# A gated attention-and-feed-forward layer on one core: another order of loads and instructions, a mask table, idle transposes, and the last batch's feed-forward by halves

## The chip, the cores and the metric

The kernel runs on one core of a Trainium2 chip, written directly for the engines: TensorE (PE) multiplies and transposes, VectorE (DVE), ScalarE (ACT) and GpSimd (POOL) do elementwise work, SyncE (SP) issues most DMAs. The metric is the time of one execution on the device in microseconds; lower is better. A time given for a kernel is the median of its runs.

## What is computed

x and ctx are 8 batches of 512 tokens by 256 features. The weights are wq, wk, wv, wo (256x256), pos_bias (512x512), w1 (256x1024), w2 (1024x256), w_gate, w_up (1024x256) and w_down (256x1024), with their bias rows. All is float32.

```
def aft_local(emb, ...):                 # T = 512 tokens, window S = 64
    q, k, v = emb @ wq + bq, emb @ wk + bk, emb @ wv + bv
    mask = abs(i - j) < 64
    w = pos_bias * mask                  # zero outside the band, still summed
    ek, ew = exp(k - max_over_tokens(k)), exp(w - max_over_j(w))
    num, den = ew @ (ek * v), ew @ ek    # ew is 512x512
    return (sigmoid(q) * num / den) @ wo + bo

def block1(x, ctx):
    emb = layer_norm(x) + ctx
    a   = layer_norm(aft_local(emb) + emb) * gamma + beta
    ff  = relu(a @ w1 + b1) @ w2 + b2
    return layer_norm(ff + a) * gamma + beta

def block2(x):                           # int8-like activations, ternary weights
    bit(x, w) = quantised(x) @ quantised(w).T
    # weight scale: mean(|w|), then round and clip to -1, 0, 1
    return bit(silu(bit(x, w_gate)) * bit(x, w_up), w_down)

x = x + tanh(g_xattn) * block1(layernorm(x), ctx)
x = x + tanh(g_ffn)   * block2(layernorm(x))
```

## The kernel before

**Tiling.** A batch is four tiles of 128 tokens. Work goes batch by batch in a software pipeline: while TensorE does the feed-forward products of batch b, the other engines prepare the attention of batch b+1 and the second block of batch b-1 or b-2. Every fp32 product is split: each operand has an upper part (`_hi`, written by ScalarE) and a lower part (`_lo`, the rest, written by VectorE), and three products hi·hi, lo·hi and hi·lo are added (helper `product`, L2444). So each operand passes PSUM, ScalarE, VectorE, and back to TensorE.

**Order.** There is no scheduler: for each engine a list of calls is written out by hand, such as `hidden(0, 3)`, and semaphore counts tie the lists together. An engine runs its list strictly in order, so a call that waits holds everything behind it. PSUM has eight banks; the table `BANK` says which bank each step of each batch uses, and `bank_wait` makes TensorE wait until the bank's last reader is through.

**Steps of the first block,** in their order per batch, with the line that the profile shows. Layer norm: `tile_stats` (DVE L1550), `mean_variance` (L1558), `rsqrt` on GpSimd (L530 to L535), `normalise` (ACT L847). `embed` adds ctx (POOL L540). `emb_rows` transposes it (PE L2452), `emb_upper` and `emb_lower` split it (ACT L861, DVE L1563). `keys_T` and `max_row` (L2461, L2478) give the largest key per feature, used by `bias` (DVE L1584). `queries` and `keys_values` are products (L2444) with wq and with wk, wv; `half_sigmoid` (ACT L868), `add_bias` (DVE L1591), `exp_keys` (ACT L874), `weighted` (DVE L1597) and `e_upper`, `e_lower` (ACT L881, DVE L1602) follow. `attend` multiplies the banded part of ew with ek and ek*v, 256 columns at a time; outside the band ew is constant per row, so `key_sums` (L2510), `sum_upper` and `sum_lower` (ACT L888, DVE L1607) and `attend_far` (L2518) add the rest. `gated`, `inverse` (DVE L1611), `divided` and `y_upper`, `y_lower` (ACT L894, DVE L1628) finish, `project` multiplies with wo. After the next layer norm, `n1_rows` transposes (L2535), `n1_upper` and `n1_lower` split (ACT L900, DVE L1640), and `hidden(b, m)`, m from 0 to 7, makes 128 of the 1024 hidden features for all 512 tokens; `hidden_upper`, `hidden_whole` (ACT L907, L912) and `hidden_lower` (DVE L1646) feed `feed_forward(b, m)`. h_hi and h_lo are rings of four.

**Tables made once, early.** `positions_T` transposes exp(w - max) (PE L2411), after the band's zeros are set (`masks`, POOL L504, L507), the row maximum is taken (`position_max`, DVE L1496) and the exponential (`exp_positions`, ACT L810); `ewT_upper`, `ewT_lower` split it (ACT L815, DVE L1504), `far_row` and `far_weights` make the constant part. `beta_w1` (PE L2428) and `b1_whole` give beta @ w1 + b1. The weights are split by `wkv_upper` (ACT L777), `wkv_lower` (DVE L1476), `w1_upper`, `w1_lower` (ACT L798, DVE L1490) and so on. Each of w_gate, w_up, w_down (n = 0, 1, 2) is quantised by `sum_of_magnitudes` (ACT L822), `bit_scale` (DVE), `bit_round` (ACT L829), `bit_clip` (DVE L1539), `bit_whole` (ACT L837) and a DMA transpose `bit_rows`.

**Second block.** `second_residual`, layer norm, `n2_gamma` (POOL L572), `first_sum` (POOL L579, which writes the tile `x1`, one buffer for all batches), layer norm, `token_quantise` (ACT L919), the transposed activations (by DMA, and on TensorE for batch 7), `gate` and `up` (PE L2592), `silu`, `product` and `product_scale` (DVE L1683 to L1701), the quantised product, `down` (PE L2614) and `output(b, t)` (DVE L1707), which reads x1 and writes the result.

## Time and profile before

| what | value |
|---|---|
| median of 3 runs | 529.32 us |
| lowest and highest | 527.03 and 531.65 us |
| the profiled execution | 531.71 us |
| its span | 530.0 us |
| busy, share of the span: PE, DVE, ACT, POOL | 90%, 82%, 70%, 46% |
| the chain that ended last, by engine | PE 17%, ACT 4%, DMA 4%, issue 3%, POOL 2%, DVE 2% |

The profile is of one execution. Its span runs from the first to the last recorded instruction; the execution's own time is 1.7 us longer. Busy shares are averages over stages that differ, so the rows below are read by stretch and not by share. In a timeline row, the numbers are the start and the length in us, then the engine, the line of the kernel, the operation, what it writes and reads, and in square brackets how long the engine had been idle and who released it. A row of busy time per stretch has start and end, the length, the busy time and (x) the instructions of PE, PEld (weight loads), DVE, ACT and POOL, then the granted TensorE clock, the busy share of the DMA engines and GB/s; where it was asked for TensorE alone, only that engine stands in it.

### The profile page before, as it was taken

What the parts mean: (1) busy time and instruction counts of PE and PEld (TensorE: products, weight loads), DVE (VectorE), ACT (ScalarE), POOL (GpSimd) and SP (SyncE); (2) the same over time, 40 slices, a digit from 0 to 9 for tenths busy, and PEclk for the clock granted to TensorE, in tenths of its full rate; (3) what the DMA queues carried; (4) which work ended last, traced back from release to release, by engine and by line L of the source; (5) the groups of instructions that cost most, each with busy time, mean ns of one, the idle gap of its engine ahead of it and who ended that gap; (6) DMA issues with size and microseconds to landing.
All of it is one profiled execution on the core that took longest, in us unless ns stands there. A gap on an engine that the chain in (4) does not pass through costs nothing. (4 is left out here: it accounts for less than half of the span.)

```text
span 530.0 us, 9499 instructions
## 1 busy us (share of the span) xinstructions
PE 478.4 (90%) x2912; PEld 390.5 (74%) x2912; DVE 432.7 (82%) x992; ACT 372.8 (70%) x594; POOL 245.8 (46%) x386
## 2 busy tenths in 40 slices
PE   0499579999999999999999999999999999897394
PEld 0389468998887888779877888788778987775132
DVE  3676985958798989898989898998899789768474
ACT  2467874556868957886788769787768776886563
POOL 2863016318712575354743484348415903574410
PEclk9997998999999999999999999999999999999577
DMA  5965142101301233023302331222123202232301
GB/s 175 276 205 179 28 69 64 41 0 41 80 22 21 61 90 91 16 54 91 90 12 40 80 92 51 40 62 76 44 41 81 61 0 39 61 71 52 79 0 41
DMA packets 69328, 36.01 MB, mean 68 GB/s; under 512 B 47008, under 2 KB 68768, under 8 KB 69280
## 3 DMA queue, kind: packets, MB, share of 16 engines
q1 hardware_dynamic: 68160, 35.14, 26.1%
q8 instruction: 25, 0.41, 0.3%
q10 hardware_dynamic: 1120, 0.27, 0.2%
q14 instruction: 23, 0.19, 0.1%
HBM read 20.46 MB, written 4.19 MB: 47 GB/s over the span
## 5 line engine op out<-in xcount | busy, mean ns | idle before, releaser
L530 POOL TENSOR_TENSOR mv<-mv,cols 128x2 f32<-128x2 f32 x64 | 12.5, 195 | 176.6 <-DVE mv L1558 176.6
L2444 PE MATMUL ps<-w_hi,h_hi 128*128 128x256 f32 x256 | 75.8, 296 | 0.0
L2444 PE MATMUL ps<-w_lo,h_hi 128*128 128x256 f32 x256 | 71.6, 280 | 0.0
L2444 PE MATMUL ps<-w_hi,h_lo 128*128 128x256 f32 x256 | 71.5, 279 | 0.0
L907 ACT ACTIVATE h_hi<-ps,cols 128x512 fp32r<-128x512 f32 x64 | 43.8, 685 | 19.8 <-PE ps L2444 15.5
L1611 DVE RECIPROCAL ps<-ps 128x512 f32<-128x512 f32 x16 | 53.6, 3355 | 0.6 <-PE ps L2518 0.6
L2444 PE MATMUL ps<-n1T_hi,w_hi 128*128 128x512 f32 x128 | 51.3, 401 | 0.8 <-DVE n1T_lo L1640 0.8
L2444 PE MATMUL ps<-n1T_lo,w_hi 128*128 128x512 f32 x128 | 50.6, 396 | 0.0
L2444 PE MATMUL ps<-n1T_hi,w_lo 128*128 128x512 f32 x128 | 50.6, 395 | 0.0
L2444 PEld LDWEIGHTS ps<-w_hi,h_hi 128*128 128x128 f32 x256 | 48.3, 189 | 2.8 <-DVE h_lo L1646 0.2
L2444 PEld LDWEIGHTS ps<-w_lo,h_hi 128*128 128x128 f32 x256 | 48.3, 188 | 1.1
L1646 DVE TENSOR_TENSOR h_lo<-ps,h_hi 128x512 fp32r<-128x512 f32 x64 | 42.6, 682 | 7.5 <-ACT ps L912 7.1
L2444 PEld LDWEIGHTS ps<-w_hi,h_lo 128*128 128x128 f32 x256 | 48.2, 188 | 0.0
L1683 DVE TENSOR_TENSOR work<-work,ps 128x1024 f32<-128x1024 f32 x32 | 38.9, 1215 | 11.1 <-issue 8.1
L2614 PE MATMUL ps<-wdT,w_bit 128*128 128x256 bf16 x256 | 36.7, 291 | 12.1 <-DMA w_bit<-place_c 8.2
L847 ACT ACTIVATE work<-work,nmr,rstd 128x256 f32<-128x256 f32 x64 | 34.9, 595 | 14.3 <-POOL nmr L535 14.2
L953 ACT ACTIVATE work<-ps,cols 128x1024 f32<-128x1024 f32 x32 | 35.6, 1112 | 13.2 <-DVE work L1683 7.7
L533 POOL TENSOR_TENSOR rstd<-mv,cols 128x2 f32<-128x2 f32 x64 | 44.5, 695 | 0.0
L1550 DVE BATCH_NORM_STATS2 st<-work 128x6 f32<-128x256 f32 x96 | 36.5, 414 | 9.6 <-POOL work L579 9.2
L2444 PE MATMUL ps<-ew_hi,e_hi 128*128 128x256 f32 x128 | 38.6, 302 | 3.6 <-DVE e_lo L1602 3.2
L912 ACT ACTIVATE ps<-ps,cols 128x512 f32<-128x512 f32 x64 | 41.9, 657 | 0.0
L2614 PEld LDWEIGHTS ps<-wdT,w_bit 128*128 128x128 bf16 x256 | 24.3, 103 | 23.0 <-DMA w_bit<-place_c 11.2
(175 smaller groups left out, 1460.9 us busy)
## 6 DMA issues: line engine op xcount, KB each, us to landing
emb<-in_ctx_dram SPq DMA_DIRECT2D x16, 256.0 KB, 3.1
x_in<-in_x_dram SPq DMA_DIRECT2D x16, 256.0 KB, 2.9
work<-in_x_dram SPq DMA_DIRECT2D x8, 512.0 KB, 3.9
out_dram<-work SPq DMA_DIRECT2D x16, 256.0 KB, 2.1
work<-in_L_xattn_w_dram SPq DMA_DIRECT2D x2, 1024.0 KB, 8.4
work<-in_L_ffn_w_gate_dram SPq DMA_DIRECT2D x1, 1024.0 KB, 5.6
work<-in_L_ffn_w_up_dram SPq DMA_DIRECT2D x1, 1024.0 KB, 5.6
place_c<-in_L_ffn_w_down_dram SPq DMA_DIRECT2D x1, 1024.0 KB, 4.9
```

What stands on the lines that cost most here:

```text
L530: pool.tensor_tensor(mv[:, n, c, 1], mv[:, n, c, 1], eps_col[:, c], ALU.add).then_inc(power_step[n].sem, 1)
L533: pool.tensor_tensor(rstd[:, n, c], mv[:, n, c, 1], minus_half[:, c], ALU.pow).then_inc(power_step[n].sem, 1)
L847: last = nc.scalar.activation(dst[:, t, :], src[:, t, :], ACT.Identity, bias=nmr[:, n, t:t + 1], scale=rstd[:, n, t:t + 1])
L907: nc.scalar.activation(h_hi[:, m % RING, :], bank(b, "h", m), ACT.Relu, bias=b1_col[:, m:m + 1]).then_inc(h_hi_ok.sem, 1)
L912: nc.scalar.activation(bank(b, "h", m), bank(b, "h", m), ACT.Relu, bias=b1_col[:, m:m + 1]).then_inc(h_relu_ok.sem, 1)
L953: nc.scalar.activation(sg, bank_pair(b, "gate", t), ACT.Silu, scale=sgate[:, t:t + 1]).then_inc(sg_ok.sem, 1)
L1550: nc.vector.bn_stats(st6[:, n, t, :], src[:, t, :]).then_inc(stats[n].sem, 1)
L1611: nc.vector.reciprocal(bank(b, "den", h), bank(b, "den", h)).then_inc(rden_ok.sem, 1)
L1646: nc.vector.tensor_tensor(h_lo[:, m % RING, :], bank(b, "h", m), h_hi[:, m % RING, :], ALU.subtract).then_inc(h_lo_ok.sem, 1)
L1683: nc.vector.tensor_tensor(prod[t % 2].rearrange("p (a n) -> p a n", a=2), sg.rearrange("p (a n) -> p a n", a=2), bank_pair(b, "up", t), AL ...
L2444: last = nc.tensor.matmul(dst, lhsT, rhs, start=(i == 0 and not begun), stop=(i == n - 1 and ends))
L2614: last = nc.tensor.matmul(bank(b, "down", t)[:, 0:D].rearrange("p (k n) -> p k n", n=P), hqT[t % 2][:, k, :], wdT[:].rearrange("p (k j) n ...
```

## The change

**Loads.** x and ctx of batch 0 are fetched first, then the weights wq, wo, wk, wv, then the two bias rows bk and bv (`fetch_bias`, moved from ScalarE's queue to SyncE's), and the positions only after those. w1 is fetched after w2 and, by a new semaphore `masked`, not before both halves of the mask are applied. w_up and w_down are fetched after `bit_rows(0)`.

Here is how SyncE's list begins before; `place_c` holds the positions, `work` takes the weights.

```order
L338 DMA place_c<-in_L_xattn_pos_bias_dram 128x2x384
L305 DMA emb<-in_ctx_dram 128x2x256
L299 DMA x_in<-in_x_dram 128x2x256
L305 DMA emb<-in_ctx_dram 128x2x256
L299 DMA x_in<-in_x_dram 128x2x256
L338 DMA work<-in_L_xattn_wk_dram 128x2x256
L338 DMA work<-in_L_xattn_wv_dram 128x2x256
L338 DMA bo_all<-in_L_xattn_bo_dram 128x256
```

And after:

```order
L316 DMA x_in<-in_x_dram 128x2x256
L322 DMA emb<-in_ctx_dram 128x2x256
L316 DMA x_in<-in_x_dram 128x2x256
L322 DMA emb<-in_ctx_dram 128x2x256
L355 DMA work<-in_L_xattn_wq_dram 128x2x256
L355 DMA work<-in_L_xattn_wo_dram 128x2x256
L355 DMA work<-in_L_xattn_wk_dram 128x2x256
L355 DMA work<-in_L_xattn_wv_dram 128x2x256
L355 DMA bk_all<-in_L_xattn_bk_dram 128x256
L355 DMA bias_all<-in_L_xattn_bv_dram 128x256
L316 DMA x_in<-in_x_dram 128x2x256
L355 DMA place_c<-in_L_xattn_pos_bias_dram 128x2x384 x2
```

The positions went from the first place to the twelfth row, and both halves of x stand ahead of every weight.

**The mask.** GpSimd no longer writes zeros into the loaded positions. `band(h)` fills a table `in_band` with ones and sets zeros in it by two selects, which needs no load; `position_max` on VectorE multiplies the positions by it and then takes the maximum.

**Idle transposes.** TensorE runs 50 transposes of the identity into bank 7 before its first useful one. Their result is never read. The `queries` of batch 0 now stand ahead of all `keys_values`, and `positions_T` and `beta_w1` later.

TensorE's list begins so before; `ident` is the identity, `embT` the transposed emb.

```order
L2411 MATMUL ps<-ident,place_c 128x128 x2
L2452 MATMUL ps<-ident,emb 128x128 x8
L2461 MATMUL ps<-embT_hi,wkv_hi 128x512 x4
L2444 MATMUL ps<-wkv_hi,embT_hi 128x512
L2444 MATMUL ps<-wkv_lo,embT_hi 128x512
L2444 MATMUL ps<-wkv_hi,embT_lo 128x512
```

And after:

```order
L2686 MATMUL ps<-ident 128x128 x50
L2509 MATMUL ps<-ident,emb 128x128 x8
L2518 MATMUL ps<-embT_hi,wkv_hi 128x512 x4
L2501 MATMUL ps<-embT_hi,wq_hi 128x512
L2501 MATMUL ps<-embT_lo,wq_hi 128x512
L2501 MATMUL ps<-embT_hi,wq_lo 128x512
```

In front of emb's eight transposes the two of the positions are gone and the 50 idle ones stand; behind `keys_T` come products with wq and no longer with wk and wv.

**Quantised weights.** Only w_gate is quantised before batch 1's attention. The steps for w_up and w_down now stand between the hidden products of batch 0, on ScalarE, VectorE and TensorE (`total`). w1 and w2 are split in two calls each, later.

ScalarE's list after batch 0's keys, before. L822 is `sum_of_magnitudes`, L829 `bit_round`, L888 `sum_upper(0)`, L861 `emb_upper(1, h)`.

```order
L822 ACTIVATE wdT,cols<-work 128x2048
L888 ACTIVATE esum<-ps 128x512
L822 ACTIVATE wdT,cols<-work 128x2048
L861 ACTIVATE embT_hi<-ps 128x512
L829 ACTIVATE work<-work,cols 128x2048
L822 ACTIVATE wdT,cols<-place_c 128x2048
L861 ACTIVATE embT_hi<-ps 128x512
L829 ACTIVATE work<-work,cols 128x2048
```

After, in batch 0's hidden stage. L845 is `sum_of_magnitudes`, L931 and L936 are `hidden_upper` and `hidden_whole`, L917 `y_upper(1, 0)`.

```order
L936 ACTIVATE ps<-ps,cols 128x512
L845 ACTIVATE wdT,cols<-work 128x2048
L931 ACTIVATE h_hi<-ps,cols 128x512
L917 ACTIVATE y_hi<-ps 128x512
L936 ACTIVATE ps<-ps,cols 128x512
L845 ACTIVATE wdT,cols<-place_c 128x2048
L931 ACTIVATE h_hi<-ps,cols 128x512
```

The second and third sums stood around batch 1's first `emb_upper`; now they stand between batch 0's `hidden_upper` calls.

**n1 by token halves.** `n1_rows`, `n1_upper`, `n1_lower` take a pair of token tiles and both feature halves, in all batches, where before they took a feature half and all tokens.

**The last batch by halves.** For batch 7 (`HALVED`) `hidden` runs for tokens 0 to 255 with m from 0 to 7 and then for tokens 256 to 511, and `feed_pair` after it; each half starts as soon as its own n1 is there, and `second_residual` waits for its own half.

**The tail.** GpSimd runs `first_sum(7, 0)` straight behind `n2_gamma(7, 0)`; `gate(7, 2)` stands before `up(7, 2)`; on VectorE `output(7, 1)` stands before `product_scale(7, 3)`.

GpSimd's list near its end, before. L572 is `n2_gamma` (the first for batch 7, tiles 0 and 1), L579 `first_sum(7, 0)`, L584 and L585 `quantise`, L530 to L535 `rsqrt`.

```order
L572 TENSOR_TENSOR work<-work,g_all 128x512
L584 TENSOR_TENSOR cols<-cols 1x1
L585 TENSOR_SCALAR work<-work,cols 128x1024
L530 TENSOR_TENSOR mv<-mv,cols 128x2
L531 TENSOR_TENSOR mv<-mv,cols 128x2
L533 TENSOR_TENSOR rstd<-mv,cols 128x2
L535 TENSOR_TENSOR nmr<-mv,rstd 128x2
L572 TENSOR_TENSOR work<-work,g_all 128x512
L579 TENSOR_TENSOR work<-work 128x512
```

After (L596 `n2_gamma`, L603 `first_sum`):

```order
L608 TENSOR_TENSOR cols<-cols 1x1
L609 TENSOR_SCALAR work<-work,cols 128x1024
L596 TENSOR_TENSOR work<-work,g_all 128x512
L603 TENSOR_TENSOR work<-work 128x512
L554 TENSOR_TENSOR mv<-mv,cols 128x2
L555 TENSOR_TENSOR mv<-mv,cols 128x2
L557 TENSOR_TENSOR rstd<-mv,cols 128x2
L559 TENSOR_TENSOR nmr<-mv,rstd 128x2
```

`first_sum(7, 0)` no longer stands behind a `rsqrt` and the second `n2_gamma`.

Between the ends, in batches 1 to 6, neighbouring calls change places, of which the one used below is on VectorE: `y_lower(b, 1)` stands behind `hidden_lower(b-1, 5)` and `hidden_lower(b-1, 6)` and not ahead of them. The `BANK` table is new throughout. The core of the diff:

```diff
-VECTORS1, VECTORS2 = 6, 7
+VECTORS1, VECTORS2 = 4, 7
+WARM_UP = 50
+HALVED = (7,)
+HALF = (slice(0, 2 * P), slice(2 * P, T))
...
-    ("embT", 0): (0, 4, 4, 1, 0, 2, 4, 0), ("embT", 1): (1, 5, 2, 1, 7, 7, 7, 7), ("kT", 0): (0, 1, 2, 7, 7, 7, 7, 4),
+    ("embT", 0): (0, 7, 6, 5, 0, 4, 0, 4), ("embT", 1): (1, 3, 7, 0, 7, 6, 7, 6), ("kT", 0): (2, 1, 1, 5, 3, 3, 3, 0),
...
+            def fetch_bias():
+                fetch("bias", bk_all[:], bk[None, :].to_broadcast([P, D]))
+                fetch("bias", bias_all[:, D:2 * D], bv[None, :].to_broadcast([P, D]))
+
             def fetch_w1():
+                sp.wait_ge(masked, 2)
                 fetch("w1", raw_w1, w1.rearrange("(k p) n -> p k n", p=P))
...
-            def masks(h):
-                w = half(raw_pos, h)[:, :, KEYS[h][0]:KEYS[h][1]]
-                pool.wait_ge(load[f"pos{h}"], 16)
+            def band(h):
+                c, n, w = KEYS[h][0], KEYS[h][1] - KEYS[h][0], in_band[:, 2 * h:2 * h + 2, :]
+                pool.memset(w, 1.0).then_inc(mask_ok, 1)
+                pool.wait_ge(mask_ok, 3 * h + 1)
                 pool.affine_select(out=w, in_=w, compare_op=ALU.is_ge, fill=0.0, ...
...
             def position_max(h):
-                dve.wait_ge(mask_ok, 2 * h + 2)
+                w = half(raw_pos, h)[:, :, KEYS[h][0]:KEYS[h][1]]
+                dve.wait_ge(load[f"pos{h}"], 16)
+                dve.wait_ge(mask_ok, 3 * h + 3)
+                nc.vector.tensor_tensor(w, w, in_band[:, 2 * h:2 * h + 2, :], ALU.mult).then_inc(masked, 1)
+                dve.wait_ge(masked, h + 1)
+                nc.vector.tensor_reduce(wmax[:, 2 * h:2 * h + 2], w,
                                         AX.X, ALU.max).then_inc(wmax_ok, 1)
...
-            def hidden(b, m):
-                wait(pe, n1T_lo_ok, b, 2)
+            def hidden(b, m, p=0, c=slice(0, T)):
+                wait(pe, n1T_lo_ok, b, p + 1 if b in HALVED else 2)
                 pe.wait_ge(lo_ok["w1"], ND)
-                bank_wait(b, "h", m)
-                product(bank(b, "h", m), [(w1_hi[:, k, c], w1_lo[:, k, c], n1T_hi[:, k, :], n1T_lo[:, k, :])
+                bank_wait(b, "g" if p else "h", m)
+                product(h_bank(b, m, p)[:, c], [(w1_hi[:, k, r], w1_lo[:, k, r], n1T_hi[:, k, c], n1T_lo[:, k, c])
...
+            def feed_pair(b, m, p):
+                wait(pe, h_lo_ok, b, NH * p + m + 1)
+                if m == 0:
+                    bank_wait(b, "f", p)
+                feed_tiles(b, m, (2 * p, 2 * p + 1)).then_inc(f_ps.sem, 1)
...
             pe.wait_ge(const_ok, 5)
+            for _ in range(WARM_UP):
+                nc.tensor.transpose(ps[:, 7, 0:P], ident[:], ident[:])
             pe.wait_ge(dve_const_ok, 5)
-            positions_T(0)
             emb_rows(0, 0)
             emb_rows(0, 1)
             keys_T(0, 0)
             keys_T(0, 1)
+            queries(0, 0)
+            queries(0, 1)
+            max_row(0)
             keys_values(0, 0)
...
             y_lower(4, 0)
-            token_max(2, 1)
-            y_lower(4, 1)
...
             hidden_lower(3, 5)
             hidden_lower(3, 6)
+            y_lower(4, 1)
...
             n2_gamma(7, 0)
-            quantise(6, 2)
+            first_sum(7, 0)
             rsqrt(7, 2, 1)
+            rsqrt(7, 3, 0)
             n2_gamma(7, 1)
-            first_sum(7, 0)
```

## Rows read from the trace of the kernel before

**Rows 1.** Busy time per stretch: all engines
```profile
0.00:90.00 90.00, 61.51 (x323) 51.74 (x324) 61.84 (x143) 52.56 (x79) 39.54 (x59) 0.94 0.51 141
90.00:480.00 390.00, 387.08 (x2430) 323.05 (x2429) 340.90 (x772) 293.11 (x481) 192.64 (x301) 1.00 0.22 54
480.00:530.00 50.00, 29.80 (x163) 15.68 (x162) 29.98 (x79) 27.09 (x35) 13.61 (x26) 0.73 0.18 43
90.00:130.00 40.00, 39.99 (x255) 35.54 (x254) 32.14 (x75) 24.68 (x45) 16.28 (x31) 1.00 0.10 29
```

**Rows 2.** Timeline of TensorE at the start
```profile
11.78 0.66 PE L2411 MATMUL ps<-ident,place_c 128*128 128x128 f32 x2 [11.78 <-ACT place_c L810]
19.42 1.97 PE L2452 MATMUL ps<-ident,emb 128*128 128x128 f32 x8 [6.98 <-POOL emb L540]
```

**Rows 3.** TensorE's busy time per stretch, two stretches of 128x512 products
```profile
24.17:28.28 4.11, 4.11 (x9) 1.00 1.09 374
28.28:30.39 2.11, 2.11 (x11) 1.00 0.80 315
```

**Rows 4.** Timeline of VectorE at the start
```profile
8.36 0.75 DVE L1550 BATCH_NORM_STATS2 st<-x_in 128x6 f32<-128x256 f32 x2 [4.31 <-DMA x_in<-in_x_dram]
13.56 0.75 DVE L1550 BATCH_NORM_STATS2 st<-x_in 128x6 f32<-128x256 f32 x2 [3.08 <-DMA x_in<-in_x_dram]
16.00 2.25 DVE L1476 TENSOR_TENSOR wkv_lo<-work,wkv_hi 128x1024 fp32r<-128x1024 f32 x1 [1.40 <-ACT wkv_hi L777]
```

**Rows 5.** Timeline from 31 to 50 us
```profile
31.56 1.29 DVE L1591 TENSOR_TENSOR kv_f<-ps,bias_all 128x512 f32<-128x512 f32 x2
...
35.50 4.17 PE L2428 MATMUL ps<-cols,work 128*128 128x1 f32 x32
...
36.09 2.46 DVE L1490 SCALAR_TENSOR_TENSOR w_lo<-work,cols,w_hi 128x1024 fp32r<-128x1024 f32 x2
...
42.26 0.38 ACT L815 ACTIVATE ew_hi<-ps 128x256 fp32r<-128x256 f32 x1 [4.68 <-PE ps L2411]
...
49.57 0.69 DVE L1607 TENSOR_TENSOR esum<-ps,esum 32x512 fp32r<-32x512 f32 x1 [0.25 <-ACT esum L888]
```

**Rows 6.** Lines by form: ns min/median/max, first to last start, form and count
```profile
L1539 DVE TENSOR_SCALAR work<-work x2: 1215/1216/1216, 59.1 to 65.3; 128x2048 f32<-128x2048 f32 x2
...
L822 ACT ACTIVATE wdT<-work x2: 1898/1900/1903, 46.2 to 49.4; 128x2048 bf16<-128x2048 f32 x2
```

**Rows 7.** Loads: KB each and median us from issue to landing
```profile
work<-in_L_ffn_w_up_dram SPq DMA_DIRECT2D x1, 1024.0 KB, 5.6
```

**Rows 8.** Timeline from 63 to 88 us
```profile
63.90 0.47 PE L2444 MATMUL ps<-wkv_hi,embT_hi 128*128 128x512 f32 x1 [3.15 <-ACT work L868]
...
79.26 0.51 PE L2444 MATMUL ps<-ew_hi,e_hi 128*128 128x256 f32 x1 [2.36 <-DVE e_lo L1602]
79.28 0.66 DVE L1602 TENSOR_TENSOR e_lo<-ps,e_hi 128x512 fp32r<-128x512 f32 x1
...
87.58 0.47 PE L2444 MATMUL ps<-n1T_hi,w_hi 128*128 128x512 f32 x1
```

**Rows 9.** TensorE's busy time per stretch, around batch 1's key sums
```profile
79.26:83.82 4.56, 4.56 (x18) 0.63 0.41 78
83.82:84.88 1.06, 1.06 (x10) 1.00 0.00 0
```

**Rows 10.** Timeline around the projection of batch 4
```profile
262.18 0.68 DVE L1628 TENSOR_TENSOR y_lo<-ps,y_hi 128x512 fp32r<-128x512 f32 x1
...
263.04 0.36 PE L2444 MATMUL ps<-wo_hi,y_hi 128*128 128x256 f32 x1
```

**Rows 11.** Timeline of the tail
```profile
491.61 0.86 DVE L1707 SCALAR_TENSOR_TENSOR work<-ps,cols,work 128x256 f32<-128x256 f32 x2
...
493.53 1.27 POOL L579 TENSOR_TENSOR work<-work 128x512 f32<-128x512 f32 x1
...
499.91 0.47 DVE L1707 SCALAR_TENSOR_TENSOR work<-ps,cols,work 128x256 f32<-128x256 f32 x1
```

More of the change, by code:

```diff
@@ L1582, in bias @@
                 wait(dve, mrow_ps, b, 1)
+                dve.wait_ge(load["bias"], 32)
                 wait(dve, kvb_ok, b, 0)
@@ L2780, in _ @@
             max_row(3)
-            queries(3, 1)
+            feed_forward(1, 5)
             gate(0, 2)
@@ L3085, in _ @@
             attend_far(7, "num", 0)
-            attend_far(7, "den", 0)
-            feed_forward(6, 2)
+            hidden(6, 2)
             attend(7, "den", 1, 2)
+            attend(7, "den", 1, 3)
+            attend_far(7, "den", 1)
             attend(7, "num", 1, 1)
```

1146 lines of the change are left out of this document (598 added, 548 removed), and 19 rows, old and new, of the table BANK.

## The prediction

> **What bounds the kernel now.** I read the busy time by stretch first [rows 1]. From 90 to 480 us TensorE is busy for 387.08 of 390 us at the full clock, so nothing that only re-orders work there can win more than 3 us. The two ends are different: in the first 90 us TensorE is idle for 28.5 us, in the last 50 for 20.2 us, and the granted clock there means 0.94 and 0.73. The timeline then says what is late at the ends.
>
> At the start the matmuls wait 6.98 us for `emb` [rows 2]. Ahead of it stand the second half of x (VectorE waits 3.08 us for it until 13.56) and additions on GpSimd [rows 4]. Then nine 128x512 products start in 4.11 us, 0.46 us each, and from 28.28 nine more in 2.11 us, 0.23 each (the count of 11 holds two that reach over the edges) [rows 3]. That is 1.2 and then 2.4 GHz, though the clock column reads 1.00 in both: this early I read the clock from spacing. From 31.56, where batch 0's first `add_bias` runs on VectorE [rows 5], the chain is mostly VectorE's: e_lo, the position tables, the key sums (ended at 50.26, 49.57 + 0.69), the division, then the same for batch 1, ending with the last e_lo(1,3) at 79.94 (79.28 + 0.66) [rows 5, 8]. The weight-quantisation steps (sum of magnitudes, round, clip, whole) are packed in between [rows 6]. At 87.58 the first hidden product of batch 0 starts [rows 8], and TensorE is full from there.
>
> **Part 1, loads, mask and ScalarE's order up to `add_bias(0,0)` (31.56).** x and ctx of batch 0 now go first, without the 384 KB of positions and without the two bias rows on ScalarE's queue. Before, the load issued third (x's first half) was there at 8.36 and the fifth (its second half) at 13.56 [rows 4]. Now the second half of x is third: there at about 8.5. From its landing to the transposes of emb it took 19.42 - 13.56 = 5.9 us [rows 2, 4]; `normalise(0,0,1)` now also stands behind `wq_upper`, which waits for the fifth load. With 0.2 for that, the transposes of emb run at 14.6: 4.8 us earlier. The mask costs GpSimd two fills and four selects before x is there: nothing. It costs VectorE two products of 768 elements. A 1024-element product takes 2.46 / 2 = 1.23 us [rows 5], so about 0.9 us each. `keys_T`, both `queries` and `max_row` now run before any `keys_values`: 4 + 12 products, of which I take ten at 0.45 and six at 0.23, so 17.0 + 5.9 + 0.6 = 23.5, and `bias(0)` at 24. Behind it stand `mean_variance` (0.3) and `position_max(1)` (0.9 + 0.9 + 0.3): `add_bias(0,0)` at 26.7. Term: **-4.9 us**, from -7 to 0 (weights as late as before, wkv_lo at 16.00 [rows 4]).
>
> The 50 idle transposes start at about 1.6. A transpose of this shape takes about 0.25 us at the low level (8 in 1.97 [rows 2]), so they end between 7 and 14, before the 14.6. They take nothing. Do they give the full clock? After two transposes at 11.78 and 6.98 us idle the next products ran at 1.2 GHz [rows 2, 3]; after 2.36 us idle at 79.26 they did too, with a granted clock of 0.63 [rows 8, 9]. With 1 to 7 us of idle time behind the last idle transpose I expect the low level again, so zero. By a warm start instead, 8 x 0.1 + 10 x 0.22 = 3.0 us would be saved; that is a rival. The Trainium skill (TensorE: Matmul & The Clock Gate, "HAM oscillation") says that an idle gap throttles the clock again, which speaks against this edit; the 6.98 us of this trace agree, and the sum is the same without the page.
>
> **Part 2, from `add_bias(0,0)` to batch 0's key sums (31.56 to 50.26).** Before, this took 18.7 us. VectorE's own work in it, without w1's lower half (2.46 us [rows 5]), is four `add_bias` of 0.6 (1.29 for two [rows 5]), four e_lo of 0.6, four products of 0.33, four lower tables of 0.36, statistics (0.9) and 2.1 for the far weights: 10.6 us. The rest was TensorE's and ScalarE's doing: `beta_w1` held TensorE for 4.17 us ahead of the products, and ScalarE waited 4.68 us for the position tables [rows 5]. Now w1 and `beta_w1` come later and all tables are transposed before the first `attend`. I keep 2.4 us of waits between the engines: 13.0 us, **-5.7 us** (-7 to -3).
>
> **Part 3, from there to e_lo(1,3) (50.26 to 79.94).** Two clips of 1.22 us [rows 6] leave VectorE, as do two short scales (0.7) and 1.9 us of idle time; half of w1 (1.2), b1, statistics (1.0) and a wait for the first numerator (1.1) come in: -1.5. TensorE now has gaps of some 2 us here and will run `queries(1)` and `keys_values(1)` in part at 1.2 GHz. The row for that is the stretch from 79.26: nine products of 256 columns and eight of 512 took 4.56 us [rows 9]; at 0.12 (nine in 1.06 [rows 9]) and 0.23 they take 2.9, so 1.7 us are lost. I charge 1.5. Term: **0 us** (-3 to +3).
>
> **Part 4, to the feed-forward of batch 0.** ScalarE gets what left part 3: two sums of magnitudes (1.90 each [rows 6]), and two rounds and two wholes of the same 2048 elements, together 12 us, among the hidden products. From 90 to 130 us ScalarE is busy for 24.68 of 40 us and VectorE for 32.14 [rows 1]; with 12 and 2.5 more, 37 and 35 of 40 fit. The loads of w_up and w_down now wait for w1's lower half, about 70, and need 5.6 us [rows 7]: there before `sum_of_magnitudes(1)` at 77. I find no product that waits for these steps by more than 0.3 us. The 1.7 us of low clock in front of the key sums disappear and the last heads' products (0.8) come behind the first hidden ones, which moves work, not time. Term: **-1.5 us** (-2 to +4).
>
> **Part 5, the middle.** The batch order is changed in small ways. The place with the least room: `y_lower(b,1)` of batch 4 ended at 262.86 (262.18 + 0.68) and `project` started at 263.04 [rows 10]. It now stands behind two more h_lo (0.6 each) and a later reciprocal; I get 264.8. TensorE reaches `project` after one more group of transposes and one more `feed_forward` (0.4 + 1.4): 264.85. It just fits. Term **+0.5** (-1 to +6).
>
> **Part 6, the tail.** A half of tokens costs TensorE nothing: 256 columns follow each other at 0.12 us and 512 at 0.23 [rows 3, 9]. ScalarE pays 16 x 0.12, VectorE 16 x 0.06 us, beside TensorE's work. Batch 7's first half now finishes early, but x1 has one buffer: `first_sum(7,0)` needs `output(6,1)` (491.61 + 0.86 = 492.47) and ran at 493.53 behind an `n2_gamma` [rows 11]. It goes ahead of it now: -1.0. The second half needs `output(6,3)`, which ended at 500.38 (499.91 + 0.47 [rows 11]), and from there SiLU, product, maximum and scale per tile are a chain of VectorE and ScalarE to the end. gate before up gives up to 0.9, the earlier start 1, and `product_scale(7,3)` behind `output(7,1)` takes 0.5 back. Term **-1.5 us** (-3 to +1).
>
> **Sum.** -4.9 - 5.7 + 0 - 1.5 + 0.5 - 1.5 = -13.1 us. The profiled execution took 531.71 (span 530.0), so 518.6. It lay 2.4 us above the median 529.32 of the three runs (527.03 to 531.65); against the median: 516.2, rounded to **516.5**.
>
> **The rivals.**
> (a) The start comes earlier but is handed back: the quantisation steps meet batch 0's hidden stage. h_hi and h_lo pass through one in-order queue each, and a 2 us step ahead of them costs as much. With three of the six steps uncovered, +6, the time is 522.5. Against it: 15 us of room on ScalarE [rows 1].
> (b) The loads gain nothing, because many transfers share the queues: part 1 is 0, the time is 521.4.
> (c) The idle transposes hold the clock: 3.0 us more, 513.5. For it: a gap of 3.15 us at 63.90 was followed by a 128x512 product of 0.47 us, the full level [rows 8].
> (d) Slower: `project` waits for y_lo in each of the five middle batches. It decides from a wait of 2.6 us per batch, where 5 x 2.6 = 13 us eats the gain. Such a wait dropped the clock at 79.26 and cost 1.7 more [rows 8, 9]; 5 x (2.4 + 1.7) = 20.5 gives 537. For it: the room is 0.1 us by my reckoning. Against it: VectorE would have to be 2.4 us later than its rows.
> wkv_lo, 1024 elements with both inputs in SBUF, took 2.25 us beside `embed` [rows 4], against 1.23 alone. If both mask products met GpSimd's work they would cost 1.5 us more, inside part 1's bounds; in my order GpSimd waits then. The Trainium skill (SBUF — State Buffer, "Who interferes with whom") says the same of a VectorE instruction with two SBUF inputs and a GpSimd one that reads; the row agrees.
>
> **How the numbers follow.** Forecast 0.62, (c) 0.10, (a) 0.12, (b) 0.10, (d) 0.06. The bounds of the parts together, less than their plain sum since they are independent, give 516.5 + 7 and - 5.5; this takes in (a), (b) and (c), so the range is 511 to 523.5. Three runs tell a change from none at about 1%, 5.3 us: below 524.0 is faster. That is the forecast, (a), (b) and (c) but for their outer parts, 0.86; (d) half decided leaves 0.09 within 1%, 0.05 slower.
>
> **What would show it.** In the profile after: emb's transposes at 14 to 16 us, the first products behind them at 0.43 to 0.46 spacing (0.23 means rival c); `add_bias(0,0)` at 25 to 28; e_lo(1,3) near 68; the first hidden product near 73; TensorE over 0.98 busy from 75 to 465. Then ScalarE's steps of 2 us lie between hidden ones with no wait of TensorE behind them, and the wait of `project` for y_lo is under 0.3 us. The last product_scale to the end is as long as before. The prediction is wrong if VectorE's stretch between the key sums of batches 0 and 1 is longer than its rows (waits for TensorE at the low clock), or if the middle has gaps.

## The result, and the profile after

The changed kernel took 511.43 us (median of 4 runs, 510.02 to 513.87), the kernel before 530.32 us in the runs beside it (527.03 to 531.65). The ratio is 0.9652, 95% interval 0.962 to 0.9684: 3.5% faster, where 2.4% was forecast. On two other chips, later, it took 512.99 against 528.82 us (0.9693, 0.9659 to 0.9727) and 511.27 against 529.27 us (0.9673, 0.9643 to 0.9703).

The two profiled executions differ by more than the medians do: 531.71 and 510.02 us, spans 530.0 and 508.3. The first lay above its median and the second below. So the trace has 21.7 us to explain where the medians have 18.9. I laid the same marks in both traces, starts of an instruction unless "end" is said:

| mark | before | after | difference | of the stretch |
|---|---|---|---|---|
| transposes of emb, batch 0 | 19.42 | 14.32 | -5.1 | |
| `add_bias(0,0)` | 31.56 | 25.33 | -6.2 | -6.2 |
| `sum_lower(0)`, end | 50.26 | 37.84 | -12.4 | -6.2 |
| last e_lo of batch 1, end | 79.94 | 65.66 | -14.3 | -1.9 |
| first hidden product of batch 0 | 87.58 | 70.91 | -16.7 | |
| first hidden product of batch 1 | 123.02 | 108.11 | -14.9 | -0.6 |
| first hidden product of batch 5 | 346.77 | 331.62 | -15.2 | -0.2 |
| first hidden product of batch 7 | 453.06 | 436.68 | -16.4 | -1.2 |
| end of the span | 530.0 | 508.3 | -21.7 | -5.3 |

The mark at batch 0's hidden product alone would mislead: it came 16.7 us earlier, but part of batch 1's attention now stands behind it, and one mark later 14.9 are left.

First the busy time per stretch, which answers to [rows 1].

```profile
0.00:75.00 75.00, 65.66 (x372) 57.17 (x373) 64.47 (x138) 42.36 (x74) 41.30 (x62) 0.91 0.54 155
75.00:465.00 390.00, 388.77 (x2480) 324.88 (x2480) 345.31 (x792) 306.82 (x504) 193.87 (x302) 1.00 0.24 57
465.00:509.00 44.00, 26.11 (x161) 15.12 (x159) 28.21 (x74) 26.33 (x35) 13.59 (x26) 0.79 0.22 49
```

The middle is as full as it was, 388.77 of 390 us, and it begins 15 us earlier. VectorE is busy for 64.47 of the first 75 us (86%), where it was for 61.84 of 90: most of what the start gained is idle time that VectorE no longer has.

The timeline of TensorE at the start answers to [rows 2, 3].

```profile
1.62 7.90 PE L2686 MATMUL ps<-ident 128*128 128x128 f32 x50 [1.62 <-POOL ident L617]
14.32 1.94 PE L2509 MATMUL ps<-ident,emb 128*128 128x128 f32 x8 [4.80 <-POOL emb L564]
...
19.24 0.63 PE L2501 MATMUL ps<-embT_lo,wq_hi 128*128 128x512 f32 x1
19.67 0.49 PE L2501 MATMUL ps<-embT_hi,wq_lo 128*128 128x512 f32 x1
20.00 0.40 PE L2501 MATMUL ps<-embT_hi,wq_hi 128*128 128x512 f32 x1
```

The 50 idle transposes end at 9.52, TensorE is idle for 4.80 us, and emb's eight transposes take 1.94 us, as long as before (1.97). The products start 0.43 us apart (19.24, 19.67) and 0.23 apart from 20.00. TensorE had been at the full level in between: of the idle transposes, 16 start in the 3.4 us up to 5.00 and 24 in the 3 us after that.

VectorE's timeline answers to [rows 4, 5, 8].

```profile
8.83 0.75 DVE L1595 BATCH_NORM_STATS2 st<-x_in 128x6 f32<-128x256 f32 x2 [1.07 <-DMA x_in<-in_x_dram]
...
23.25 0.93 DVE L1539 TENSOR_TENSOR place_c<-place_c,work 128x768 f32<-128x768 f32 x1
24.21 0.95 DVE L1541 TENSOR_REDUCE cols<-place_c 128x2 f32<-128x768 f32 x1
...
25.33 1.28 DVE L1637 TENSOR_TENSOR kv_f<-ps,bias_all 128x512 f32<-128x512 f32 x2
...
37.15 0.69 DVE L1653 TENSOR_TENSOR esum<-ps,esum 32x512 fp32r<-32x512 f32 x1 [0.63 <-ACT esum L911]
...
44.07 3.36 DVE L1657 RECIPROCAL ps<-ps 128x512 f32<-128x512 f32 x1
47.34 1.27 DVE L1608 TENSOR_TENSOR embT_lo<-ps,embT_hi 128x512 fp32r<-128x512 f32 x2
```

x's second half is there at 8.83, `add_bias` follows `position_max(1)` without a gap, and the lower part of emb for batch 1 follows the second reciprocal without one.

ScalarE's list in batch 0's hidden stage, with two of the moved steps (L845 `sum_of_magnitudes`):

```profile
75.14 1.91 ACT L845 ACTIVATE wdT<-work 128x2048 bf16<-128x2048 f32 x1
76.94 0.20 ACT L845 ACTIVATION_READ_ACCUMULATOR wdT<-work 128x1 f32 x1
77.03 0.69 ACT L931 ACTIVATE h_hi<-ps,cols 128x512 fp32r<-128x512 f32 x1
...
78.08 0.68 ACT L936 ACTIVATE ps<-ps,cols 128x512 f32<-128x512 f32 x1
78.65 1.93 ACT L845 ACTIVATE wdT<-place_c 128x2048 bf16<-128x2048 f32 x1
```

And the waits of TensorE in the changed kernel, us in total, times, longest:

```profile
PE ps L2680 <- DMA w_bit<-place_c: 6.5, 4, 2.1
PE ps L2509 <- POOL emb L564: 4.8, 1, 4.8
PE ps L2680 <- ACT w_bit L990: 4.0, 3, 1.4
PE ps L2658 <- ACT xqT L969: 2.5, 2, 1.5
PE ps L2686 <- POOL ident L617: 1.6, 1, 1.6
PE ps L2518 <- ACT embT_hi L884: 1.4, 2, 0.7
PE ps L2509 <- DVE cols L1566: 1.2, 1, 1.2
```

No wait for h_lo or y_lo is in that view. What is left stands at the two ends, most of it in the tail (L2680 is `down`, L2658 `gate` and `up`).

The place in the middle with the least room, batch 4, answers to [rows 10]:

```profile
248.74 0.68 DVE L1674 TENSOR_TENSOR y_lo<-ps,y_hi 128x512 fp32r<-128x512 f32 x1
...
249.98 0.28 PE L2501 MATMUL ps<-wo_hi,y_hi 128*128 128x256 f32 x1
```

y_lo ends at 249.42 and `project` starts at 249.98: 0.56 us of room, where it was 0.18.

The tail answers to [rows 11] (L609 `quantise(6,2)`, L596 `n2_gamma(7,0)`, L603 `first_sum`, L1755 `output`):

```profile
469.12 1.11 POOL L609 TENSOR_SCALAR work<-work,cols 128x1024 f32<-128x1024 f32 x1
470.22 1.27 POOL L596 TENSOR_TENSOR work<-work,g_all 128x512 f32<-128x512 f32 x1
...
473.00 0.48 DVE L1755 SCALAR_TENSOR_TENSOR work<-ps,cols,work 128x256 f32<-128x256 f32 x1
473.64 1.27 POOL L603 TENSOR_TENSOR work<-work 128x512 f32<-128x512 f32 x1 [2.15 <-DVE work L1755]
...
480.46 0.48 DVE L1755 SCALAR_TENSOR_TENSOR work<-ps,cols,work 128x256 f32<-128x256 f32 x1 [0.67 <-PE ps L2680]
```

`output(6,3)` ends at 480.94, 19.4 us earlier than before (500.38), where batch 7's first hidden product was 16.4 earlier. The wait of 2.15 us before `first_sum` is now for `output(6,1)` alone.

### The profile page after: what moved, and what is told of

It reads as the page before. It is cut to its first block, busy times and chain, and to the rows that moved or that the text cites. A ratio compares the mean times of both kernels' runs of the same rounds, so it can differ in the third digit from the quotient of the medians.

```text
span 508.3 us, 9743 instructions
## 1 busy us (share of the span) xinstructions
PE 480.5 (95%) x3010; PEld 397.2 (78%) x3010; DVE 438.0 (86%) x1002; ACT 375.5 (74%) x611; POOL 248.8 (49%) x389
## 4 chain that ended last, share of the span: by engine, by line
PE 83%; DVE 6%; issue 3%; DMA 3%; ACT 2%; POOL 1%; SPq 0%; DVEq 0%; POOLq 0%
PE ps L2501 60%; PE ps L2658 8%; PE ps L2680 4%; PE ps L2567 3%; PE ps L2509 2%; PE ps L2518 2%; DVE cols L1737 2%; DMA work<-in_L_xattn_wo_dram 2%; DMA w_bit<-place_c 1%; PE ps L2575 1%; PE ps L2593 1%; DVE work L1731 1%; DVE ps L1657 1%; PE ps L2535 1%; DVE st L1595 1%
## 5 line engine op out<-in xcount | busy, mean ns | idle before, releaser
L2501 PE MATMUL ps<-n1T_hi,w_hi 128*128 128x512 f32 (+1 forms) x144 | 54.1, 376 | 0.4 <-DVE n1T_lo L1686 0.3
L931 ACT ACTIVATE h_hi<-ps,cols 128x512 fp32r<-128x512 f32 (+1 forms) x72 | 45.4, 637 | 11.3 <-PE ps L2501 10.1
L2501 PE MATMUL ps<-n1T_lo,w_hi 128*128 128x512 f32 (+1 forms) x144 | 53.3, 370 | 0.0
L2501 PE MATMUL ps<-n1T_hi,w_lo 128*128 128x512 f32 (+1 forms) x144 | 53.2, 370 | 0.0
L1692 DVE TENSOR_TENSOR h_lo<-ps,h_hi 128x512 fp32r<-128x512 f32 (+1 forms) x72 | 43.8, 623 | 5.9 <-ACT ps L936 5.1
L2680 PE MATMUL ps<-wdT,w_bit 128*128 128x256 bf16 x256 | 35.3, 283 | 10.6 <-DMA w_bit<-place_c 6.5
L936 ACT ACTIVATE ps<-ps,cols 128x512 f32<-128x512 f32 (+1 forms) x72 | 43.7, 612 | 0.0
L2680 PEld LDWEIGHTS ps<-wdT,w_bit 128*128 128x128 bf16 x256 | 23.7, 100 | 19.9 <-DMA w_bit<-place_c 9.6
L1737 DVE TENSOR_REDUCE cols<-work 128x1 f32<-128x1024 f32 x32 | 38.7, 1210 | 0.3
```

The source lines that it names most:

```text
L931: nc.scalar.activation(h_hi[:, m % RING, c], h_bank(b, m, p)[:, c], ACT.Relu, bias=b1_col[:, m:m + 1]).then_inc(h_hi_ok.sem, 1)
L936: nc.scalar.activation(h_bank(b, m, p)[:, c], h_bank(b, m, p)[:, c], ACT.Relu, bias=b1_col[:, m:m + 1]).then_inc(h_relu_ok.sem, 1)
L1692: nc.vector.tensor_tensor(h_lo[:, m % RING, c], h_bank(b, m, p)[:, c], h_hi[:, m % RING, c], ALU.subtract).then_inc(h_lo_ok.sem, 1)
L1737: nc.vector.tensor_reduce(hm[:, t:t + 1], prod[t % 2], AX.X, ALU.max, apply_absolute_value=True).then_inc(hm_ok.sem, 1)
L2501: last = nc.tensor.matmul(dst, lhsT, rhs, start=(i == 0 and not begun), stop=(i == n - 1 and ends))
L2680: last = nc.tensor.matmul(bank(b, "down", t)[:, 0:D].rearrange("p (k n) -> p k n", n=P), hqT[t % 2][:, k, :], wdT[:].rearrange("p (k j) n ...
```

## The experiments

All edits are to the changed kernel. They ran in three groups, each on one chip and beside the kernel before; kernels of one group are compared with each other. The medians of the kernel before (11 runs each) were 527.4 us in the first group, 528.82 in the second and 529.27 in the third. The first group had no run of the changed kernel as it stands: there a time can be set only against the kernel before and the other edits, and a trace against traces from other chips.

### First group: the start

**No idle transposes.**

```diff
-WARM_UP = 50
+WARM_UP = 0
```

> The changed kernel without the 50 idle transposes. In the changed kernel they ran from 1.62 to 9.52 us, then TensorE was idle for 4.80 us, the products started at 0.43 us spacing and rose to 0.23 at 20.00, 5.7 us after emb's transposes began at 14.32; before, the rise came 8.9 us after them (19.42 to 28.28). Theory A (the prediction's): the idle gap takes the warm clock away again, so the transposes give nothing; time as the changed kernel within 0.5 us, the rise again about 5.7 us after emb's transposes, add_bias(0,0) still at 25.3. Theory B: they shorten the slow stretch by 3 us; without them the rise comes 8.9 us behind 14.32, at 23.2, where each 128x512 product costs 0.2 us more, nine of them, so 1 to 2 us slower.

Measured: 514.16 us (512.99 to 514.69), ratio 0.9743 (0.9709 to 0.9777). emb's transposes ran at 14.48 in 1.94 us, the products came to full spacing at 20.68, `add_bias(0,0)` at 25.77: 0.44 us later. At the start theory A holds in this trace. The rest of the time lay elsewhere in the trace (38.56 us instead of 37.20 between the first hidden products of batches 0 and 1, 57.07 instead of 56.17 in a middle batch, 73.1 instead of 71.6 behind batch 7's), with no common place. Repeated below.

**A run of idle transposes that reaches emb.**

```diff
-WARM_UP = 50
+WARM_UP = 92
```

> The changed kernel with 92 idle transposes in place of 50, so that TensorE is busy until about 14 us, when emb is there. Theory A (only an idle gap loses the clock): the gap of 4.80 us is gone, emb's eight transposes take 1.0 instead of 1.94 us and the first products follow at 0.23, so add_bias(0,0) starts 2.0 us earlier at most (its own queue on VectorE leaves less: position_max(1) ends at 25.3), and the time falls by 0.5 to 2 us. Theory B (TensorE's clock at the start does not set the end, VectorE's queue does): add_bias(0,0) stays at 25.3 and the time within 0.5 us.

Measured: 510.54 us (510.01 to 511.47), ratio 0.9682 (0.9652 to 0.9713). TensorE's timeline there:

```profile
12.79 0.71 PE L2686 MATMUL ps<-ident 128*128 128x128 f32 x5
14.24 1.06 PE L2509 MATMUL ps<-ident,emb 128*128 128x128 f32 x8 [0.74 <-POOL emb L564]
16.04 1.20 PE L2518 MATMUL ps<-embT_hi,wkv_hi 128*128 128x512 f32 x4 [0.74 <-ACT embT_hi L884]
17.12 0.47 PE L2501 MATMUL ps<-embT_hi,wq_hi 128*128 128x512 f32 x1
17.43 0.40 PE L2501 MATMUL ps<-embT_lo,wq_hi 128*128 128x512 f32 x1
```

Idle for 0.74 us instead of 4.80, TensorE runs all of it at the full level: 1.06 instead of 1.94 us for the eight transposes. `add_bias(0,0)` starts at 23.67 (-1.7), the first hidden product of batch 0 at 69.22 (-1.7). So theory A's mechanism is shown, and the 50 transposes of the changed kernel are too few for it. That the time followed is not shown: against the kernel before it is 16.9 us, where the changed kernel gained 15.8 to 18.9 on three chips, and the span is 508.5 beside 508.3.

**The mask on GpSimd.** `masks(h)` of the kernel before, behind the two `embed` calls; `position_max` without its product. The load of w1 no longer waits for the mask either.

```diff
-            band(0)
-            band(1)
...
             embed(0, 1)
+            masks(0)
+            masks(1)
             rsqrt(1, 0, 0)
...
-                nc.vector.tensor_tensor(w, w, in_band[:, 2 * h:2 * h + 2, :], ALU.mult).then_inc(masked, 1)
-                dve.wait_ge(masked, h + 1)
```

> The changed kernel, but the mask is put on the loaded positions by GpSimd's selects as before, behind the two embed calls; the table of ones and zeros and the two products on VectorE (0.94 us each) are gone. Theory A: VectorE's queue ahead of add_bias(0,0) is the bound there (the second product and maximum end at 25.3, the first keys_values pair at about 24.9), so add_bias starts up to 0.5 us earlier and the time falls by 0 to 0.5 us. Theory B: GpSimd's four selects (0.84 us each) wait for the positions and end later than the products did, the exponentials of the positions follow and attend starts later: 0.5 to 2 us slower.

Measured: 511.62 us (510.59 to 513.68), ratio 0.9705 (0.9671 to 0.9738). `add_bias(0,0)` at 24.77, but the key sums end at 38.27 and the first hidden product is at 71.63, 0.7 us later than in the first trace of the changed kernel and 0.1 later than in the last one (71.51). The last one is the fairer comparison, since TensorE came to the full level at the same time there (20.91 and 20.86): `add_bias(0,0)` is 0.95 us earlier than in it and the key sums end together (38.27 and 38.23). VectorE had less to do and waited instead (0.95 us for `exp_keys`). Building the mask as a table is worth nothing that these runs can tell.

**Positions first.**

```diff
-            fetch_x(0, 0)
+            fetch_positions(0)
             fetch_ctx(0, 0)
-            fetch_x(0, 1)
+            fetch_x(0, 0)
             fetch_ctx(0, 1)
+            fetch_x(0, 1)
             fetch_wqo()
```

> The changed kernel with the head of the load list as before: the first half of the positions, then ctx, x, ctx, x of batch 0, then the weights. Theory A (the prediction's part 1): x's second half is the fifth load again, there 4 to 5 us later, so emb's transposes start at about 18 to 19 instead of 14.3 and the time rises by 3.5 to 5 us, nearly all of the term for the loads. Theory B: VectorE's queue takes it up (position_max can run early, since the positions are there) and the time rises by 1 to 2 us.

Measured: 513.73 us (512.81 to 514.86), ratio 0.9743 (0.9711 to 0.9774); 2.1 us over the mask on GpSimd and 3.2 over the long idle run, in the same group: between the two theories. VectorE saw x's halves so:

```profile
8.83 0.75 DVE L1595 BATCH_NORM_STATS2 st<-x_in 128x6 f32<-128x256 f32 x2 [1.93 <-DMA x_in<-in_x_dram]
...
10.45 0.75 DVE L1595 BATCH_NORM_STATS2 st<-x_in 128x6 f32<-128x256 f32 x2 [0.58 <-DMA x_in<-in_x_dram]
```

The fifth load is there at 10.45, not at 13.56 as before [rows 4]; emb's transposes run at 15.88, 1.6 us later than changed and 3.5 earlier than before. `add_bias(0,0)` is 2.4 us later: TensorE also came to the full level later (23.32), and `bias(0)` waits 0.83 us for `max_row`. So the order of the first five loads is worth about 1.6 us of emb's 5.1. The other 3.5 are in what this run kept of the change. Of these, 3.1 are the landing of the fifth load (13.56 to 10.45) and 0.4 the way from there to the transposes of emb. The two bias rows off ScalarE's queue and behind the weights are the obvious candidate for the landing, but the order of the weights changed too, and no run took them apart.

### Second group: the tail

**The changed kernel again.**

> The changed kernel itself once more, beside the kernels that undo parts of its tail, so that those are compared on the same chip and in the same minutes. Both theories: within 1.5 us of the 511.4 us first measured, and a second profile, in which the stretches that are chance (gaps of TensorE for DMA transposes in the middle batches) can be told from those that are the kernel's.

Measured: 512.99 us (511.29 to 513.36). Up to batch 7's first hidden product (437.25) the marks are those of the first trace to 0.7 us.

**Batch 7 whole.** TensorE's, ScalarE's and VectorE's lists from about `down(5, 1)` on, and the banks of these steps, as before.

```diff
-HALVED = (7,)
+HALVED = ()
...
-            hidden(7, 0, 0, HALF[0])
-            hidden(7, 1, 0, HALF[0])
+            hidden(7, 0)
+            hidden(7, 1)
```

> The changed kernel with batch 7's feed-forward undone: hidden and feed_forward for all 512 tokens at a time, and TensorE's, ScalarE's and VectorE's orders from there on as before (gate and up, output and product_scale included); GpSimd's order stays as changed. The changed kernel took 71.6 us from the first hidden product of batch 7 to the end, before 76.9. Theory A (the prediction's part 6): the halves and these orders are worth about 0.5 us, since x1 has one buffer and the second half waits for output(6,3); time up by 0 to 1 us. Theory B: the halves let batch 6's last steps and batch 7's layer norm run earlier on VectorE and ScalarE; they are worth most of the 5.3 us, time up by 3 to 5 us.

Measured: 522.48 us (521.82 to 523.14), 9.5 us over the control. More than either theory gave: GpSimd's new order doesn't fit the whole batch. `first_sum(7,0)` stands ahead of `rsqrt(7, 2, 1)` in it and waits 2.02 us for `output(6,1)`, until 480.19. ScalarE then waits for that `rsqrt`, and batch 6's last quantisation (L962) stands behind it:

```profile
482.71 1.09 ACT L850 ACTIVATE work<-work,nmr,rstd 128x256 f32<-128x256 f32 x2 [4.60 <-POOL nmr L539]
483.71 1.23 ACT L962 ACTIVATE work<-work,cols 128x1024 f32<-128x1024 f32 x1
```

With GpSimd's order of before as well (the whole tail undone, below) that quantisation starts at 478.15. TensorE waits 6.11 us for the transpose that follows it, before `down(6, 3)`.

**GpSimd's tail as before, halves kept.**

```diff
             quantise(6, 0)
             rsqrt(7, 2, 0)
-            quantise(6, 2)
             n2_gamma(7, 0)
-            first_sum(7, 0)
+            quantise(6, 2)
             rsqrt(7, 2, 1)
-            rsqrt(7, 3, 0)
             n2_gamma(7, 1)
+            first_sum(7, 0)
+            rsqrt(7, 3, 0)
             first_sum(7, 1)
```

> The changed kernel with GpSimd's order in the tail as before, from the first quantise of batch 6: n2_gamma(7,0) ahead of quantise(6,2), first_sum(7,0) behind n2_gamma(7,1). The halves stay. Theory A (the prediction's): first_sum comes 1.0 us later and all behind it, time up by about 1 us. Theory B: with the halves n2_gamma(7,0) waits for batch 7's layer norm and holds quantise(6,2) behind it, which feeds batch 6's last products; time up by 2 us or more.

Measured: 516.42 us (514.92 to 519.2), 3.4 us over the control. GpSimd there:

```profile
470.69 1.27 POOL L596 TENSOR_TENSOR work<-work,g_all 128x512 f32<-128x512 f32 x1 [2.10 <-ACT work L870]
471.92 0.18 POOL L608 TENSOR_TENSOR cols<-cols 1x1 f32<-1x1 f32 x1
472.08 1.11 POOL L609 TENSOR_SCALAR work<-work,cols 128x1024 f32<-128x1024 f32 x1
```

and in the control, whose first hidden product of batch 7 is 0.08 us later:

```profile
469.71 1.11 POOL L609 TENSOR_SCALAR work<-work,cols 128x1024 f32<-128x1024 f32 x1
470.82 1.28 POOL L596 TENSOR_TENSOR work<-work,g_all 128x512 f32<-128x512 f32 x1
```

That is theory B as it was written: `n2_gamma(7,0)` waits 2.10 us for ScalarE, and `quantise(6,2)`, which waits for nothing itself, stands behind it: 472.08 instead of 469.71. `down` of batch 6, tile 2, then starts at 477.50 instead of 475.14, its wait 4.50 us instead of 2.94.

**The whole tail undone.** Both edits together.

> Both of the last two together: the tail of all four engines as before, the rest as changed. Theory A: 1 to 2 us slower than the changed kernel. Theory B: the whole 5 to 6.5 us that the traces show behind batch 5's first hidden product come back. If the two parts are independent, this is the sum of the two single runs.

Measured: 518.56 us (517.73 to 518.68), ratio 0.9802 (0.9769 to 0.9835), 5.6 us over the control. From batch 7's first hidden product to the end it took 76.7 us, as before the change (76.9); the control took 72.1. Theory B. The two parts are not independent: 9.5 and 3.4 alone, 5.6 together. The four kernels of the group as a table:

| median, us | GpSimd's order of before | GpSimd's new order |
|---|---|---|
| batch 7 whole, other engines' orders of before | 518.56 | 522.48 |
| halves, other engines' new orders | 516.42 | 512.99 |

GpSimd's order wins 3.4 us with the halves and loses 3.9 without them. The halves with GpSimd's old order are 2.1 us faster than neither, but these two intervals overlap (0.9738 to 0.9814 against 0.9769 to 0.9835), and from batch 7's first hidden product on their traces take nearly the same time (76.3 and 76.7 us).

### Third group: what was open

> The changed kernel itself, on the same chip and in the same minutes as the three kernels beside it. Within 1.5 us of 512 us.

Measured: 511.27 us (510.42 to 512.69).

**No idle transposes, again.**

> The changed kernel without the idle transposes again, now beside a control. The first run was 3 us slower than its neighbours, but its trace had add_bias(0,0) only 0.44 us later, and the rest in waits on VectorE and ScalarE in batch 0's hidden stage, one in a middle batch and in the tail. Theory A (only the start counts, the rest was chance): 0 to 0.7 us slower than the control. Theory B (0.5 us later at the start shifts the slower engines against the DMAs and costs more behind it): 2 us slower or more again, and the wait for batch 3's x in batch 0's hidden stage is there again.

Measured: 513.06 us (512.13 to 516.12), ratio 0.972 (0.9683 to 0.9758) beside 0.9673 (0.9643 to 0.9703) of the control. In its trace the products came to the full level at 22.62, `add_bias(0,0)` was at 26.54 and the first hidden product at 72.85, 1.3 us later than the control's; the wait for batch 3's x was not there, so it does not belong to the edit. The 1.8 us over the control lie between the two theories (up to 0.7, and 2 or more), with intervals that overlap; the traces place at most 1.3 of it at the start, where the moment of the full level also moves by chance (last section).

**The moved steps made short.**

```diff
+                c = slice(0, 128 if n else 2048)
-                nc.scalar.activation(... raw_bit[n].rearrange("p k n -> p (k n)"), ACT.Abs, accum_out=wsum[:, n:n + 1])
+                nc.scalar.activation(... raw_bit[n].rearrange("p k n -> p (k n)")[:, c], ACT.Abs, accum_out=wsum[:, n:n + 1])
```

and the same for round, clip and whole.

> The changed kernel with the quantisation steps of w_up and w_down (sum, round, clip, whole) done on 128 of 2048 columns only, so its weights for those two are wrong: it prices the eight steps that now lie in batch 0's hidden stage. They take 12 us of ScalarE and 2.4 us of VectorE less. Theory A (the prediction's part 4): they are covered, time as the control within 0.5 us. Theory B (rival a): TensorE waits for h_hi and h_lo behind them, time down by 1.5 us or more.

Measured: 511.66 us (510.38 to 513.21), ratio 0.9676 (0.9647 to 0.9706), the control's. From the first hidden product of batch 0 to that of batch 1, first here and then in the control:

```profile
73.21:110.28 37.07, 37.04 (x232) 32.82 (x232) 29.16 (x69) 21.92 (x44) 14.36 (x29) 1.00 0.34 92
```

```profile
71.51:108.69 37.18, 37.15 (x233) 32.81 (x233) 31.39 (x69) 30.94 (x44) 15.04 (x29) 1.00 0.37 91
```

ScalarE has 9.0 us less to do in the stretch and TensorE takes the same time, 37.07 and 37.18. Theory A: the moved steps are covered.

**Long idle run and mask on GpSimd together.**

> The changed kernel with both edits that took something off the start: 92 idle transposes, and the mask by GpSimd on the loaded positions. Alone, the first had add_bias(0,0) at 23.67 us and the first hidden product at 69.22 (25.33 and 70.91 in the changed kernel), the second had add_bias(0,0) at 24.77 and the first hidden product at 71.63. Theory A (VectorE's queue is the bound of the start once the clock is up, and 1.9 us leave it): first hidden product at 68 to 69, time 2 to 3 us below the control. Theory B (the start no longer sets the end; what it wins is given back as waits for batch DMAs in the middle, as in the first of the two): within 1 us of the control.

Measured: 510.45 us (509.52 to 511.56), ratio 0.9655 (0.9626 to 0.9684), 0.8 us under the control, with intervals that overlap. `add_bias(0,0)` was at 22.70 and the first hidden product at 68.86, 2.7 us before the control's: theory A's start. By the first hidden product of batch 5 the lead was 1.5 us (330.73 against 332.26), by batch 7's 1.0. Its trace has waits, a batch apart, that neither the control's profile nor the first one of the changed kernel has:

```profile
285.53 1.05 PE L2676 MATMUL ps<-wdT,w_bit 128*128 128x256 bf16 x8 [0.35 <-DMA w_bit<-place_c]
...
342.31 1.05 PE L2676 MATMUL ps<-wdT,w_bit 128*128 128x256 bf16 x8 [0.46 <-DMA w_bit<-place_c]
```

A batch takes 56.8 us there (217.26 to 274.02) and 56.2 in the control (219.60 to 275.78). That is theory B: an earlier start turns in part into waits for the transposed activations. The kernel with the long idle run alone had the same waits at 285.72 and 342.97. Why the DMAs are not earlier by as much was not tested.

## Why the prediction was right, and where it was off

The forecast, -13.1 us against the profiled execution, was right in sign, and in mechanism for the start, and too small: by medians 18.9 us went. The measured 511.43 us lie 0.4 us inside the stated range (511 to 523.5). Part of that is chance: the gain was 15.8 us on one of the other chips.

**Part 1: -4.9 forecast, -6.2 in the first trace (-5.8 in the last control).** The mark for emb held (14.6 forecast, 14.32 measured). The slow products numbered seven instead of ten: `keys_T`'s four and three behind them, the full level from 20.00. In other traces with the same start they number up to 14, so ten was no bad guess. In the first trace `add_bias(0,0)` is set by VectorE's own list, 25.33 behind `position_max(1)`, as the part reckoned with its 0.94 us products; in the last control `bias(0)` waits 0.40 us for TensorE ahead of that. The reason given for emb's mark, the load order, holds only for 1.6 of 5.1 us (positions first): that the fifth load lands at 13.56 because it is the fifth was a wrong reading, since in that run the fifth was there at 10.45. So the mark held partly by luck.

**The idle transposes: zero forecast.** Every trace with 50 of them shows the slow level behind the gap, and the full level back between 20.00 and 23.32; without them it was back at 20.68 and 22.62. At the start they buy nothing that stands out of this spread. Rival (c) needed a run that reaches emb, and that gives 1.7 us at `add_bias` where 3.0 was reckoned. The clock was at the full level in the idle transposes; 4.80 us idle lost it, 0.74 us did not, and neither did 3.15 us in the trace before [rows 8]. By the Trainium skill's rule (TensorE: Matmul & The Clock Gate, "HAM oscillation") an idle gap throttles the clock; the 4.80 us agree. The 6.98 us that the prediction held beside that rule could not test it, because no row shows the full level ahead of them. Whether the 50 are worth the 1.8 us of the repeated run is open.

**Part 2: -5.7 forecast, -6.2 measured.** The stretch took 12.5 us, where 13.0 was worked out from VectorE's rows and 2.4 us of waits. No run put `beta_w1` and the split of w1 back, so for this term, as large as part 1, the cause is read from the rows and not tested.

**Part 3: 0 forecast, -1.9 measured.** The low clock that was charged did come:

```profile
44.30:50.00 5.70, 5.01 (x15) 0.50 0.24 80
50.00:55.00 5.00, 5.00 (x27) 0.94 0.01 2
```

with `beta_w1` and a wait of 1.25 us just ahead. But it cost nothing: VectorE was in its reciprocal until 47.4 and took emb's transposes right behind it. The charge of 1.5 us was made for an engine that nobody waited for. What made up the 1.9 us was not taken apart.

**Part 4: -1.5 forecast, -0.6 measured,** counted to batch 1's first hidden product. Rival (a) is out: the short steps change nothing.

**Part 5: +0.5 forecast, -0.2 measured.** `project` waits in no middle batch, and its room grew to 0.56 us. The part had TensorE at 264.85 and y_lo at 264.8 without the 15 us of the start; less those, 249.85 and 249.8, and measured were 249.98 and 249.42. Rival (d) never had a start.

**Part 6: -1.5 forecast, -5.3 in the first trace behind batch 7's first hidden product.** This is the step that failed, and with 3.8 us it is the largest single part of the miss, which is 8.6 us between the profiled executions. Undone on the chip, the whole tail costs 5.6 us by medians; by the traces 4.6 of that lie behind the same mark. The part took `output(6,3)` as given, 500.38 less what the whole kernel gains, and counted only what follows it. Measured from batch 7's first hidden product, in the control:

- `output(6,3)` starts 43.8 us behind it instead of 46.85: -3.0. In the kernel before, `product(6,2)` on VectorE stood behind `second_residual(7,1)`, which waited 0.96 us for the last feed-forward product of all 512 tokens. `quantise(6,2)` on GpSimd ran behind `n2_gamma(7,0)` but lost nothing by that place, since it then still waited 0.35 us for VectorE (L1698):

```profile
484.05 0.69 DVE L1656 TENSOR_TENSOR work<-ps,work 128x512 f32<-128x512 f32 x1 [0.96 <-PE ps L2444]
484.65 1.21 DVE L1683 TENSOR_TENSOR work<-work,ps 128x1024 f32<-128x1024 f32 x1
...
488.10 0.18 POOL L584 TENSOR_TENSOR cols<-cols 1x1 f32<-1x1 f32 x1 [0.35 <-DVE cols L1698]
488.27 1.11 POOL L585 TENSOR_SCALAR work<-work,cols 128x1024 f32<-128x1024 f32 x1
```

  With halves `product(6,2)` starts 28.7 us behind the mark instead of 31.6 (465.96 in the control), with either order on GpSimd. Only then does GpSimd's order decide whether this is passed on: `quantise(6,2)` starts at 32.5 with the new one, at 34.9 with the old one, and at 35.2 in the kernel before. The diff shows this move beside the one of `first_sum`, and the prediction counted only the latter.
- from there to `product(7,3)` 16.35 us instead of 17.5: -1.1. The wait of 0.56 us for SiLU ahead of `product(7,2)` is gone; that gate going before up did this is the likely reading, not tested alone.
- from `product(7,3)` to the last output 8.8 instead of 9.5: -0.7. `output(7,1)` ahead of `product_scale(7,3)` was charged 0.5. VectorE did finish that scale 0.4 us later behind `product(7,3)` (3.7 instead of 3.35), but the last transposes, which waited 0.67 us for an output before, wait for one no longer.

So it takes both: the halves bring batch 6's last products forward, and GpSimd's order lets them through.

The rest of the profiled difference, 1.2 us between batches 5 and 7, also went when the tail was undone (106.8 us from batch 5's to batch 7's first hidden product, 105.4 in its control). By medians the three comparisons give 15.8 to 18.9 us.
